# A macaron layer (FFN, attention, FFN) on one core: the order of the attention's side work is rearranged

## The reference

```
x = q                                         # (8, 512, 256) float32, 8 sequences
x = x + 0.5 * ffn(layernorm(x))               # FFN a
x = x + attention(layernorm(x))               # 16 heads of 16, ALiBi bias -slope*|i-j|, softmax, Wo, bo
x = x + 0.5 * ffn(layernorm(x))               # FFN c
ffn(x) = (silu(x @ wg.T) * (x @ wu.T)) @ wd.T # hidden size 768, weights are int / 127
```

## Time and profile before

| what | value |
|---|---|
| median of 3 runs | 875.68 us (873.27 to 876.71) |
| the profiled execution, its own time | 872.84 us |
| its span | 871.0 us |
| PE, DVE, ACT, POOL busy | 92%, 74%, 60%, 49% of the span |
| FFN a, from the start to the first score | 198.2 us |
| attention, first score to the first product of FFN c | 513.3 us |
| FFN c, from there to the end of the span | 159.5 us |

### The profile page before, as it was taken

The page is one execution under the profiler, slowest core; times in us unless marked ns, Lnnn a source line. Parts: engine busy times, 40 slices in busy tenths (PEclk is TensorE's granted clock), DMA queues, the critical chain, the costliest instruction groups (busy, mean ns, idle before and its releaser), DMA issues.

```text
span 871.0 us, 13022 instructions
## 1 busy us (share of the span) xinstructions
PE 803.0 (92%) x4576; PEld 490.4 (56%) x4576; DVE 644.1 (74%) x1347; ACT 518.3 (60%) x745; POOL 430.0 (49%) x486
## 2 busy tenths in 40 slices
PE   2699999998899999999999999999999978999997
PEld 2578887864344444444444444444443437888886
DVE  5488877867887777777777778778778726777764
ACT  4333444336578678677678678678577773444443
POOL 0343345344446646556556556556445544344433
PEclk9799999999899999999999999999899999999999
DMA  9230025303551451452351352252350000100001
GB/s 366 110 41 3 2 36 79 36 2 54 60 74 22 54 74 28 48 75 33 43 75 30 46 75 38 38 75 35 40 69 7 2 2 3 50 26 27 26 26 50
DMA packets 21491, 43.18 MB, mean 50 GB/s; under 512 B 3848, under 2 KB 5912, under 8 KB 21208
## 3 DMA queue, kind: packets, MB, share of 16 engines
q1 hardware_dynamic: 21400, 41.92, 28.1%
HBM read 12.02 MB, written 4.62 MB: 19 GB/s over the span
## 4 chain that ended last, share of the span: by engine, by line
PE 64%; DVE 25%; DMA 4%; issue 3%; SPq 2%; POOL 1%; ACT 1%; DVEq 0%; ACTq 0%
PE ps L952 61%; DVE row_max L821 13%; DVE hid L756 3%; DMA q_scale<-q_scale 2%; DVE max_in L831 2%; DMA q_aug<-max_row 2%; PE ps L964 1%; DVE newton L688 1%; DVE max_in L833 1%; PE ps L1010 1%; DVE xn L711 1%; DVE var L680 1%; DVE xnt L877 1%; SPq L361 1%; DVE mean_var L670 1%
## 5 line engine op out<-in xcount | busy, mean ns | idle before, releaser
L821 DVE TENSOR_REDUCE row_max<-ps 128x1 f32<-128x512 f32 x512 | 329.1, 685 | 110.1 <-PE ps L952 109.4
L644 ACT ACTIVATE probs<-ps 128x1024 f32<-128x1024 f32 x256 | 260.1, 1026 | 48.2 <-PE ps L952 47.8
L522 POOL TENSOR_TENSOR probs<-probs,diag 128x256 f32<-128x256 f32 x256 | 191.0, 750 | 179.7 <-ACT probs L644 179.3
L452 POOL TENSOR_TENSOR hid_r<-hid,hid_r 128x512 fp32r<-128x512 f32 x96 | 124.8, 1301 | 192.2 <-ACT hid_r L549 191.3
L952 PE MATMUL ps<-xnt,wgu_r 128*128 128x512 f32 x768 | 193.9, 406 | 16.8 <-DVE hid L756 12.6
L952 PEld LDWEIGHTS ps<-xnt,wgu_r 128*128 128x128 f32 x768 | 144.4, 192 | 57.9 <-DVE hid L756 17.9
L952 PE MATMUL ps<-k_aug,q_aug 60*128 60x512 f32 x512 | 153.1, 435 | 16.3 <-DVE row_max L821 10.7
L952 PE MATMUL ps<-probs,v_aug 128*32 128x512 f32 x1024 | 140.4, 621 | 7.3 <-POOL probs L522 7.3
L555 ACT ACTIVATE gated<-ps 128x512 f32<-128x512 f32 x96 | 57.3, 598 | 135.2 <-PE ps L952 126.2
L952 PE MATMUL ps<-q_aug,k_aug 62*128 62x512 f32 x512 | 129.2, 500 | 2.6 <-DMA q_aug<-max_row 2.2
L952 PEld LDWEIGHTS ps<-q_aug,k_aug 62*128 62x128 f32 x512 | 48.4, 185 | 113.3 <-issue 68.0
(11 more groups left out here) (72 smaller groups left out, 654.5 us busy)
## 6 DMA issues: line engine op xcount, KB each, us to landing
q_aug<-parts SPq DMA_DIRECT2D x96, 128.0 KB, 4.2
k_aug<-parts SPq DMA_DIRECT2D x96, 128.0 KB, 5.9
x_sb<-x_in SPq DMA_DIRECT2D x8, 512.0 KB, 12.6
x_out<-x_sb SPq DMA_DIRECT2D x8, 512.0 KB, 2.6
diag<-diag_table SPq DMA_DIRECT2D x1, 2048.0 KB, 18.9
wgu_i<-w_gate_up SPq DMA_DIRECT2D x2, 768.0 KB, 6.0
w_att<-w_att SPq DMA_DIRECT2D x1, 1024.0 KB, 11.2
q_aug<-max_row SPq DMA_DIRECT2D x64, 8.0 KB
```

Of the source, the lines that this page charges most:

```text
L452: nc.gpsimd.tensor_tensor(hid_r[:, 1, f, :], hid[:, f % 2, :], hid_r[:, 0, f, :].bitcast(F32), ALU.subtract).then_inc(s["hid_lo"], 1)
L522: nc.gpsimd.tensor_tensor(tile, tile, diag[:, kt % 2, n * QH + 2 * pair:n * QH + 2 * pair + 2, :], ALU.mult).then_inc(fixed, 1)
L644: nc.scalar.activation(probs[:, kt % 2, 2 * pair:2 * pair + 2, :], ps[:, at:at + 2, :], ACT.Exp, scale=SLOPE_UNITS[pair]).then_inc(exp_don ...
L821: nc.vector.reduce_max(row_max[:, quad % 2, u % 2, u // STEPS, (u % STEPS) // 2:(u % STEPS) // 2 + 1], max_bank(tile), mybir.AxisListType. ...
```

## The change

- Odd steps are now scores, values, maxima, fill; even ones scores, maxima (and the small `max` fills at step 4). All other fills stand at odd steps, in a new order: `turn0` is made one sequence later (`turn0_prev`), `out0` and `out1` move to quad 3, `qk1`, `qk2`, `qk3` to (1, 3), (1, 7), (2, 7), and `max1` to `max0_next` from step 5 to step 4.
- The low part of `xt` is made by POOL. POOL adds `bo` tile by tile at the even steps of quad 2 and places values at (3, 4), (3, 5), (3, 6).
- DVE's normalizing goes to (1, 3), (2, 3) and (3, 1), its `first_rows` and `last_blocks` to four odd steps each, its divisions to two steps after the fill.
- The tail has five fills and is spread over turns 0, 1 and 2 of FFN c.
- The program of SP has no change.

```
 FILLS = {
-    (0, 0): "xt0_next", (0, 2): "xt1_next", (0, 4): "heads3_prev", (0, 5): "max1", (0, 6): "qk0_next",
-    (1, 0): "qk1_next", (1, 2): "turn1_prev", (1, 4): "heads0", (1, 5): "max2", (1, 6): "out0_prev",
-    (2, 0): "out1_prev", (2, 2): "v0_next", (2, 4): "heads1", (2, 5): "max3", (2, 6): "qk2_next",
-    (3, 0): "qk3_next", (3, 2): "v1_next", (3, 4): "heads2", (3, 5): "max0_next", (3, 6): "turn0",
+    (0, 1): "xt0_next", (0, 3): "xt1_next", (0, 4): "max1", (0, 5): "heads3_prev", (0, 7): "qk0_next",
+    (1, 1): "turn0_prev", (1, 3): "qk1_next", (1, 4): "max2", (1, 5): "heads0", (1, 7): "qk2_next",
+    (2, 1): "turn1_prev", (2, 3): "v0_next", (2, 4): "max3", (2, 5): "heads1", (2, 7): "qk3_next",
+    (3, 1): "v1_next", (3, 3): "out0_prev", (3, 4): "max0_next", (3, 5): "heads2", (3, 7): "out1_prev",
 }
...
 FIRST_V = 5
-LAST_BLOCKS_AT = {(2, 2): 0, (2, 3): 1, (2, 6): 2, (2, 7): 3}
+LAST_BLOCKS_AT = {(2, 3): 0, (2, 7): 1, (3, 3): 2, (3, 7): 3}
+APPLY_AT = {(1, 3): (0,), (2, 3): (1,), (3, 1): (2, 3)}
+FIRST_ROWS_C_AT = {(1, 3): 0, (2, 3): 1, (3, 1): 2, (3, 3): 3}
+PLACE_AT = {(3, 4): 0, (3, 5): 1, (3, 6): 2}
 FIRST_FILLS = [f for f in ALL_FILLS if not f.endswith("_prev")]
...
 LAST_FILLS = [f for f in ALL_FILLS if not f.endswith("_next") or f.startswith("xt")]
-TAIL_FILLS = ["heads3_prev", "turn1_prev", "out0_prev", "out1_prev"]
-
-TAIL_AT = {0: "heads3_prev", 2: "turn1_prev", 4: "out0_prev", 5: "out1_prev"}
+TAIL_FILLS = ["heads3_prev", "turn0_prev", "turn1_prev", "out0_prev", "out1_prev"]
+
+TAIL_AT = {(0, 1): "heads3_prev", (1, 1): "turn0_prev", (1, 4): "turn1_prev", (2, 1): "out0_prev", (2, 4): "out1_prev"}
...
-SPLIT_POOL, SPLIT_DVE, HEADS, OUT = ("qk", "turn"), ("xt",), ("heads",), ("out",)
-SPLIT = SPLIT_POOL + SPLIT_DVE
+SPLIT, HEADS, OUT = ("qk", "turn", "xt"), ("heads",), ("out",)
 STAGED = SPLIT + HEADS + OUT
...
         split_hi = sem("split_hi")
-        done = {kinds: sem(f"{kinds[0]}_done") for kinds in (SPLIT_POOL, SPLIT_DVE, HEADS, OUT)}
+        done = {kinds: sem(f"{kinds[0]}_done") for kinds in (SPLIT, HEADS, OUT)}
...
                 for f in range(FT):
-                    if w == 1 and first(b) and f - 1 in TAIL_AT:
-                        take(B, TAIL_AT[f - 1])
+                    if w == 1 and (b, f - 1) in TAIL_AT:
+                        take(B, TAIL_AT[b, f - 1])
                     pool.wait_ge(s["hid_hi"], FT * b + f + 1)
...
                         take(-1, FIRST_AT[b, f - 1])
-                if w == 1 and first(b):
-                    take(B, TAIL_AT[FT - 1])
                 if w == 0 and (b, FT - 1) in FIRST_AT:
...
                 nc.gpsimd.tensor_tensor(lo, stage[:, slot_of(b, name), :], hi.bitcast(F32), ALU.subtract
-                                        ).then_inc(done[SPLIT_POOL], 1)
+                                        ).then_inc(done[SPLIT], 1)
...
             def take(b, name):
-                if name.startswith(SPLIT_POOL):
+                if name.startswith(SPLIT):
                     split(b, name)
...
-            def add_bo(b):
+            def add_bo(b, tiles):
...
                     pool.wait_ge(xn_ready, TT * (B + b))
-                for tile in range(TT):
+                for tile in tiles:
                     nc.gpsimd.tensor_tensor(x_of(b, tile), x_of(b, tile), bo[:], ALU.add).then_inc(bo_added, 1)
...
-            add_bo(0)
+            add_bo(0, range(TT))
...
                             pool.wait_ge(pv_done, b * (NQ * TT))
-                        if (n, s) == (3, 7) and not last(b):
-                            pool.wait_ge(pv_done, b * (NQ * TT) + 3 * TT)
+                        if (n, s) in PLACE_AT and not last(b):
+                            pool.wait_ge(pv_done, b * (NQ * TT) + (PLACE_AT[n, s] + 1) * TT)
                             pool.wait_ge(drained, fill_no(b, "v1_next") + 1)
...
                         if not last(b):
-                            if (n, s) == (1, 0):
-                                add_bo(b + 1)
-                            if (n, s) == (3, 7):
-                                for quad in range(3):
-                                    place_v(b + 1, quad)
+                            if n == 2 and s % 2 == 0:
+                                add_bo(b + 1, (s // 2,))
+                            if (n, s) in PLACE_AT:
+                                place_v(b + 1, PLACE_AT[n, s])
                         name = FILLS.get((n, s))
...
                         hidden_hi(f - 1)
-                    if w == 1 and first(b) and f - 1 in TAIL_AT:
-                        drain(B, TAIL_AT[f - 1])
+                    if w == 1 and (b, f - 1) in TAIL_AT:
+                        drain(B, TAIL_AT[b, f - 1])
                     if w == 0 and (b, f - 1) == FIRST_TURN_AT:
...
                     drain(-1, FIRST_AT[b, FT - 1])
-                if w == 1 and first(b):
-                    drain(B, TAIL_AT[FT - 1])
                 if not last(b):
...
                         row_maxima(0, FIRST_MAX_AT[b, f])
-                    if w == 1 and first(b) and f == 1:
-                        divide(B, TAIL_AT[0])
+                    if w == 1 and (b, f - 1) in TAIL_AT and TAIL_AT[b, f - 1].startswith(HEADS):
+                        divide(B, TAIL_AT[b, f - 1])
+                if w == 1 and b == B - 3:
+                    wait_done(dve, B, TAIL_FILLS[-1])
                 if b < B - 2:
...
                         apply_kept(1, (at, at + 1))
-                if w == 1 and first(b):
-                    wait_done(dve, B, TAIL_FILLS[-1])
                 for j in range(2):
...
-            def split(b, name):
-
-                hi, lo = hi_and_lo(name)
-                dve.wait_ge(split_hi, count_before(b, name, SPLIT) + 1)
-                nc.vector.tensor_tensor(lo, stage[:, slot_of(b, name), :], hi.bitcast(F32), ALU.subtract
-                                        ).then_inc(done[SPLIT_DVE], 1)
-
             def divide(b, name):
...
                 else:
+                    dve.wait_ge(filled, fill_no(B - 2, "xt1_next") + 1)
                     ln_apply(at, 0, range(TT))
...
                     for s in range(STEPS):
-                        if n == 1 and 2 <= s < 6:
-                            if b + 2 < B:
-                                apply_kept(b + 2, (s - 2,))
-                            elif b + 2 == B:
-                                first_rows(s - 2)
+                        row_maxima(b, max_tiles_at(b, n * STEPS + s))
+                        name = FILLS.get((n, s - 2))
+                        if name in fills_of(b) and name.startswith(HEADS):
+                            divide(b, name)
                         if first(b) and (n, s) in LAST_BLOCKS_AT:
                             last_blocks(LAST_BLOCKS_AT[n, s])
-                        row_maxima(b, max_tiles_at(b, n * STEPS + s))
-                        name = FILLS.get((n, s - 1))
-                        if name in fills_of(b) and name.startswith(HEADS):
-                            divide(b, name)
-                        if name in fills_of(b) and name.startswith(SPLIT_DVE):
-                            split(b, name)
+                        if b + 2 < B and (n, s) in APPLY_AT:
+                            dve.wait_ge(filled, fill_no(b, "xt1_next") + 1)
+                            apply_kept(b + 2, APPLY_AT[n, s])
+                        if b + 2 == B and (n, s) in FIRST_ROWS_C_AT:
+                            first_rows(FIRST_ROWS_C_AT[n, s])
...
                     if halves[0] == 0:
-                        wait_done(pe, b, "heads1" if part == 0 else "heads3_prev")
+                        wait_done(pe, *((seq, "heads1") if part == 0 else (b, "heads3_prev")))
                     for t in tiles:
...
                 wait(pe, s["y_used"], 2 * b)
-                if w == 1 and first(b):
-                    pe.wait_ge(drained, fill_no(B, TAIL_FILLS[-1]) + 1)
+                if w == 1 and b in [at[0] for at in TAIL_AT]:
+                    pe.wait_ge(drained, fill_no(B, [TAIL_AT[at] for at in TAIL_AT if at[0] == b][-1]) + 1)
                 either(lambda weights, r: down(weights[1], r, w, b))
...
                         ins.then_inc(s[done], 1)
-                    if w == 1 and first(b) and f in TAIL_AT:
-                        fill(B, TAIL_AT[f])
+                    if w == 1 and (b, f) in TAIL_AT:
+                        wait(pe, s["y_used"], 2 * b)
+                        fill(B, TAIL_AT[b, f])
                     if w == 0 and (b, f) == FIRST_TURN_AT:
...
                         name = FILLS.get((n, s))
-                        scores_for_max(b, max_tiles_at(b, n * STEPS + s))
                         if s > 1 and s % 2 == 1:
...
                             weigh_values(quad_no - 1, (n - 1) % NQ, TT - 1, b)
-                        if first(b) and (n, s) == (0, 0):
+                        scores_for_max(b, max_tiles_at(b, n * STEPS + s))
+                        if first(b) and (n, s) == (0, 1):
```

## The result

The changed kernel takes 908.68 us (median of 4 runs, 906.34 to 912.97) against 874.47 us of the kernel before (4 runs, 872.75 to 876.71): a ratio of 1.0400, 95% interval 1.0363 to 1.0436. It is slower, which was held to be the likeliest, but by 34 us and not by 9.5, and outside the range.

What follows compares the result with a forecast made beforehand. No one engine bounded the kernel, but a cycle of short waits. +17.2 (sequences 1 to 5) +1.5 (6) -1.5 (0) -5.0 (7) -2.7 (tail) = +9.5 us on 872.84 gave 882.3 us, range 860 to 893.

Steps and rivals of the forecast that it cites:

- the hole: Start of quad 2, sequences 0 to 6: PE idle 3.7 us each, max2's rows landing behind qk1's six moves.
- the half clock behind it: Quad 2 after the idle PE: time at 1.2 GHz costs 1.6 us, within bounds 0 and 3.45.
- the wait for heads_t: Quad 1, values of key tile 0: PE waits 0.7 us, the drained fill lying just ahead of heads_t on ACT.
- quad 1: Middle sequences: 19.6 us from scores to scores, 15.9 without the late landing, against 17.34 before; no wait for POOL.
- The first rival: Start of quad 2: the 8 KB maxima moves pass the large ones, so it starts on time; 845 us, chance 0.13.
- the second: Rival for quads 0 to 2: heads_t comes in time, saving 18 us over 7 sequences; 864 us, chance 0.12.
- The third: Rival: each wait for heads_t also brings half clock, another 3 us a sequence; about 904 us, chance 0.08.
- 13.3 + 13.2 + 10.9 + 13.1 = 50.5: Sequence 7 by quads, without moves and with DVE free of xt: 50.5 us against 55.49, so -5.0.
- 63.7: Sequence 0, without "prev" fills: 63.7 us against 65.24, so -1.5.
- 68.2 each: Sequences 1 to 5: 15.2 + 19.6 + 17.2 + 16.2 by quads, 341.0 us together against 323.82, so +17.2.
- Sequence 6: 70.2 us against 68.74, so +1.5; DVE's statistics hide in quad 1 and cost some 2 us in quads 2 and 3.
- the closing fills: Tail, turns 0 to 2 of FFN c: five fills cost 6.1 us against 8.85 for four, so -2.7; turns some 19 to 22.

Runs made afterwards that it cites:

- the first run: Changed kernel, with SP moving max2 ahead of qk1's six moves: 872.58 us, ratio 1.0002 to the kernel before.
- the fourth: Kernel before the change, with SP holding qk1's six moves until the scores of step (1, 6) are done: 920.98 us, ratio 1.0568.
- the second run: Changed kernel, with ACT copying heads_t after the exp of step 1, ahead of the drain of that step's fill: 895.10 us, ratio 1.0269.
- The eleventh run: On the tenth, DVE reduces half of each maxima tile of the last sequence once more, into an unread buffer: 869.69 us, ratio 0.9968.
- the seventh: On The third version, odd steps of the last sequence alone have maxima ahead of values again: 862.90 us, ratio 0.9863.
- the sixth run: On The third version, DVE's statistics of the last two sequences are made in six pieces instead of four: 857.83 us, ratio 0.9782.
- The third version: Changed kernel with the edits of the first run and the second run together: 863.68 us, ratio 0.9907.
- eighth: On The third version, the low part of xt is made by DVE again instead of POOL: 859.36 us, ratio 0.9819.
- The fifth: On The third version, the five closing fills stand one in each of turns 0 to 4 of FFN c: 860.68 us, ratio 0.9815.
- twelfth: On the tenth, all five closing fills stand in turn 0 of FFN c: 856.15 us, ratio 0.9802.
- the tenth: On the kernel of the sixth run, POOL's bias adds of quad 2 stand at the odd steps: 856.24 us, ratio 0.9798.
- the ninth: On the kernel of the sixth run, every odd step has maxima ahead of values again, fills unmoved: 934.15 us, ratio 1.0696.

## Why the prediction was right and wrong

**Right: the hole, its cause and its size.** "3.7 us of idle PE in each of sequences 0 to 6" came out at 23.7 us in 7 waits, 3.4 each. Its cause was put on SP's unchanged program; moving one call there takes it away (the first run), and holding the same moves back makes it in the old kernel (the fourth). The 8.7 us of a group of six and the landing in order were both read from the earlier trace rows. The Trainium skill (DMA: Bandwidth & Descriptors, Queues, rings and completion order), which the prediction quoted for the case against it, says that completion is not FIFO per issuing engine. The landing shown above, 4.12 us after issue and 0.2 us behind the sixth large move, does not show a small DMA passing. The same section says that a semaphore's increment lands only after every earlier write of that SDMA engine, and by that sentence the trace agrees.

**Right: the half clock behind it**, 1.3 us (sequences 3, 4 and 6, 3.4 us at half clock each) or 2.1 us (sequences 2 and 5, 6.8 us) where 1.6 was taken. The 1.6 was the middle of wide bounds, so its closeness is partly luck: sequence 1 had no half clock in quad 2. **Right: the wait for heads_t**, 15.7 us in 28 waits; the second run gives 13.6 back. **Right: quad 1**, 19.58 for 19.6, and the wait for POOL in it is gone; but the landing sets that length, and without the hole the quad takes 16.09 for 15.9 (the first run). The first rival, that the maxima pass, and the second, that heads_t is in time, fell by the rows of the waits. The third, half clock wherever PE waits, came nearest in its number, 904, but the middle sequences show half clock behind the hole alone; in sequence 7 there was half clock behind a wait for heads_t.

**Wrong: sequence 7 (the step "13.3 + 13.2 + 10.9 + 13.1 = 50.5").** It missed by 9.6. It was priced from PE's pieces and ACT's queue with "DVE is free of xt", and DVE was given no price of its own where the fills of 1.59 are gone, although the working of quad 1 says that without those fills DVE's and POOL's work would be "0.2 to 0.5 us on PE" each. The second version has neither a late heads_t nor half clock in this sequence, and shows its bare pace: 13.42, 14.77, 13.25 and 13.26, in all 54.7. Quads 0 and 3 were priced rightly, quads 1 and 2 are 1.57 and 2.35 us too low. Timelines of DVE and PE, after, at the start of quad 1:

```profile
699.81 1.29 DVE L818 TENSOR_REDUCE row_max<-ps 128x1 f32<-128x512 f32 x2 [0.96 <-PE ps L941]
701.01 0.24 DVE L875 RECIPROCAL den<-stage 128x16 f32<-128x16 f32 x1
701.29 0.88 DVE L877 TENSOR_TENSOR heads<-stage,den 128x256 f32<-128x256 f32 x1
702.09 2.55 DVE L818 TENSOR_REDUCE row_max<-ps 128x1 f32<-128x512 f32 x4
```

```profile
700.55 1.10 PE L941 MATMUL ps<-k_aug,q_aug 60*128 60x512 f32 x2 [0.54 <-DVE row_max L818]
```

The division of heads, 1.1 us, stands between two pairs of reductions, PE has no bank to fill, and no long fill covers it. The first two steps take 1.54 and 3.27 us here and 1.54 and 3.29 in quad 2, for 0.57 and 2.56 in quad 0, which a long fill precedes. In quad 2 PE also waits 1.46 us at step 4 for DVE's negated maxima. This is read from the timelines; no run moved the division. The late heads_t and the half clock come on top, as PE's timeline shows:

```profile
708.68 1.09 PE L941 MATMUL ps<-k_aug,q_aug 60*128 60x512 f32 x2 [0.55 <-DVE row_max L818]
710.20 0.27 PE L999 MATMUL ps<-eye,max_in 128*32 128x128 f32 x1 [0.42 <-DVE max_in L830]
...
711.12 1.93 PE L941 MATMUL ps<-probs,v_aug 128*32 128x512 f32 x8
...
723.96 1.93 PE L941 MATMUL ps<-probs,v_aug 128*32 128x512 f32 x8 [0.97 <-ACT heads_t L627]
```

So of the 9.6 us, 4.2 are the bare pace of the steps, put too low in quads 1 and 2, and 5.4 are the waits for heads_t (0.58, 0.97 and 0.97) and the clock, which the sum for sequence 7 does not name. The eleventh run shows that DVE's time counts in those two quads and hardly in quad 0; the seventh shows that the old order of maxima and values would be no better, 57.0 at full clock.

**Wrong: sequences 0 and 1 (the steps "63.7" and "68.2 each").** They missed by 5.8 and by 4.7 (72.87 for 68.2). The first sequences were given no price for DVE's statistics; the trace puts the cost past the boundary, at the start of sequence 1, and the sixth run takes 3.4 us of it back. In sequence 0 quads 2 and 3 take 19.14 and 16.14 for 16.3 and 14.5, at a granted 0.76 and 0.89:

```profile
230.08:249.22 19.14, 18.66 (x89) 7.93 (x89) 12.53 (x25) 9.56 (x12) 8.47 (x12) 0.76 0.20 33
249.22:265.36 16.14, 14.59 (x82) 6.45 (x83) 12.68 (x34) 10.56 (x14) 6.81 (x10) 0.89 0.46 63
```

The third version has neither the hole nor half clock in this sequence and takes 61.6 us (15.41, 15.39, 16.23, 14.57), where the forecast without its 5.3 for hole and clock is 58.4. So 3.2 of the 5.8 are the pace of the steps, priced too low in quads 0 to 2. The rest goes with the half clock, 13.7 us of it in this sequence where some 6.9 was reckoned with. Half clock does not need the hole there: in the first version and the sixth to eighth, which have no hole, quad 2 has a stretch of it and takes 17.5.

**Wrong in size: the other sequences.** Sequences 2 to 5 take 69.0 to 69.9 for 68.2: quad 0 15.68 for 15.2, quad 3 16.48 for 16.2, quad 2 up to 18.2 for 17.2. Each term is small, together 4.9 us. Sequence 6 came out near, 69.67 for 70.2, by two misses that cancel: DVE's statistics made it 0.5 us longer than sequence 4 and not 2, and the rest was put 1.0 too low.

**Wrong in size: the closing fills**, -0.75 for -2.7, in the forecast's own band of 19 to 22 us a turn save for 22.42: the five fills cost 8.1 us over three turns of 18.40, where 6.1 was forecast. The fifth and twelfth runs show that the number of turns hardly matters.

In one sentence: the loss was found and sized, 37 us for 36, and the gains it was set against (27 us, from 872.6 to 845) were not there, and 20 of the 24 us that were missed lie in the first two sequences and the last, where DVE's work without a long fill to cover it, and half clock behind short waits, had been given no price.

## What to carry to other kernels

Where fills are moved, read every queue written out by hand beside them: a DMA of 8 KB that the next stage waits for, issued behind six of 128 KB, came 3.5 us late seven times, and one call moved on SP was worth 4% of the kernel. On the engine that drains, put what PE waits for next ahead of what is needed later, another 1 to 1.5%. And price the first and the last pass of a loop by themselves, engine by engine: a step without a long fill is paced by whatever that fill covered.

The new order of the steps itself is worth keeping. With the two orders mended, the statistics spread and the bias moved, the kernel takes about 856 us (the tenth and twelfth versions, 0.980 of the time before, 0.975 to 0.986), and with the old order of the steps 934 (the ninth).

## What the runs showed of the hardware that was not expected

**Half clock doesn't follow each hole.** Seven holes of the changed kernel look alike, but quad 2 takes 17.39 to 18.19 us behind those of sequences 2 to 6 and 16.06 behind that of sequence 1, where the granted clock is 1.00:

```profile
305.70:321.76 16.06, 15.35 (x93) 7.28 (x93) 11.15 (x21) 10.56 (x14) 9.72 (x13) 1.00 0.23 37
```

What sets it apart was not found. Half clock also appears where PE has only short waits: 0.55, 0.42 and 0.97 us in sequence 7, as shown above.

**Turn 1 of FFN c takes 21.3 us or 25.3 to 27.0**, in executions with the same closing fills: 21.3 in the changed kernel and in the seventh, eighth and ninth versions, 25.3 to 27.0 in the first, second, third, sixth, tenth and eleventh. In these six PE stands still once among the down products, 2.1 to 2.7 us, in the other four never. The profile names POOL's hid_r for it. The sixth version's row of waits and its stretch of half clock, which begins within that wait:

```profile
PE ps L940 <- POOL hid_r L455: 2.7, 1, 2.7
```

```profile
731.90:738.70 6.80, 5.75 (x28) 5.74 (x28) 0.00 (x0) 0.43 (x1) 0.44 (x1) 0.50 0.01 2
```

But POOL isn't late. The product that waits is the fifth of the down products, which needs the low part of f = 0; in the sixth version POOL had made that by 720.19, and PE waits from 730.24 to 732.96. What does differ is the queue that the profile calls instruction (q8). In each of the six executions a packet of 16 KB starts there 34.95 to 35.10 us after turn 0's first product, takes about 1 us, and PE stops at 35.1; in the four others that packet comes at 27.6, and PE doesn't stop. So PE probably waits for code there. Ten traces agree on that, and no run moved the packet. The stop moves a single execution by some 4 us, so that spans of single executions don't rank versions that lie closer than that; the medians do.
